# A decoder block in one kernel: a scan and a reciprocal of the WKV tail a slot later, four gaps in SBUF, and a divided last norm

## The reference

```python
x = layernorm(x + attention(x))     # 16 heads of 128, 4 KV heads, RoPE, causal softmax, Wo
x = layernorm(x + wkv(w, u, x, ctx))
x = layernorm(x + ffn(x))

# wkv, per channel, over the positions:
y  = (A * p + E * vt) / (A * q + E)
p, q = A2 * p + E2 * vt, A2 * q + E2

# ffn, per position:
h      = silu(x @ rw1.T + rb1)                      # 64 wide
logits = (h @ rw2.T + rb2)[:, :16] + gates
coeff  = softmax of the two largest logits, 0 elsewhere
out    = x @ W.T + bias + sum over e, r of (x . A[e, r]) * coeff[e] * B[e, :, r]
```

## Time and profile before

| | us |
|---|---|
| runs | 1602.74, 1603.10, 1606.97 (median 1603.1) |
| profiled execution, own time | 1607.82 |
| its span | 1606.0 |
| PE busy | 1556.0 (97%) |
| DVE busy | 1340.3 (83%) |
| ACT busy | 1115.5 (69%) |
| POOL busy | 1007.7 (63%) |
| mean granted TensorE clock | 0.991 |

### The profile page before, as it was taken

One profiled execution on the slowest core, in us unless ns is written; L12 is line 12 of the kernel. 1 busy time (PEld: TensorE's weight loads), 2 busy tenths in 40 slices (PEclk: granted clock), 3 DMA queues, 4 the chain that ended last, 5 costly groups with the idle time before them and its releaser, 6 DMA issues.

```text
span 1606.0 us, 32704 instructions
## 1 busy us (share of the span) xinstructions
PE 1556.0 (97%) x10500; PEld 1413.4 (88%) x10500; DVE 1340.3 (83%) x3434; ACT 1115.5 (69%) x2995; POOL 1007.7 (63%) x850
## 2 busy tenths in 40 slices
PE   8999999999999999999999999999999987989997
PEld 7899999999999999999999999999999976878785
DVE  6776688889888889898999889898989897877863
ACT  6777787877787778777877787878787865334332
POOL 2665586757675867676767666676667653635653
PEclk9999999999999999999999999999999999999999
DMA  9765344324442444244424442445144522121211
GB/s 298 256 225 201 112 150 137 116 73 142 150 137 55 152 146 136 60 152 151 139 60 152 151 139 60 132 146 164 44 126 148 178 70 79 53 93 66 80 66 53
DMA packets 81625, 202.62 MB, mean 126 GB/s; under 512 B 10416, under 2 KB 11056, under 8 KB 81456
## 3 DMA queue, kind: packets, MB, share of 16 engines
q1 hardware_dynamic: 81456, 200.53, 40.0%
HBM read 120.80 MB, written 37.75 MB: 99 GB/s over the span
## 4 chain that ended last, share of the span: by engine, by line
PE 84%; DVE 7%; issue 3%; POOL 2%; ACT 1%; DVEq 1%; DMA 1%; SPq 0%; ACTq 0%; POOLq 0%
PE bank L528 25%; PE bank L529 24%; PE bank L530 24%; PE bank L652 5%; PE bank L597 2%; PE bank L643 1%; PE bank L598 1%; PE bank L635 1%; DVE PS L1328 1%; DVE ED L1339 1%; PE bank L667 1%; DMA SW<-QB 1%; DVE SW L1392 0%; DVE RC L1170 0%; DVE OTl L1243 0%
## 5 line engine op out<-in xcount | busy, mean ns | idle before, releaser
L528 PE MATMUL bank<-Xh,W 128*128 128x256 f32 x1280 | 362.2, 283 | 5.8 <-DVE RC L1170 2.5
L529 PE MATMUL bank<-Xl,W 128*128 128x256 f32 x1280 | 360.5, 282 | 0.0
L530 PE MATMUL bank<-Xh,W 128*128 128x256 f32 x1280 | 360.4, 282 | 0.0
L1025 POOL TENSOR_TENSOR Ql<-RC,Qh 128x512 fp32r<-128x512 f32 x127 | 169.6, 1336 | 208.9 <-ACT Qh L744 208.7
L759 ACT ACTIVATE S<-S,NM 128x128 f32<-128x128 f32 (+1 forms) x512 | 228.2, 447 | 65.8 <-DVE NM L1155 65.2
L528 PEld LDWEIGHTS bank<-Xh,W 128*128 128x128 f32 x1280 | 241.3, 189 | 9.2 <-DVE RC L1170 5.1
L1013 POOL TENSOR_TENSOR SW<-SW,tables 128x512 f32<-128x512 f32 x128 | 170.8, 1334 | 124.6 <-DMA SW<-QB 124.5
L744 ACT ACTIVATE PTh<-bank 128x384 fp32r<-128x384 f32 x256 | 124.9, 488 | 173.1 <-PE bank L652 173.1
L529 PEld LDWEIGHTS bank<-Xl,W 128*128 128x128 f32 x1280 | 241.7, 189 | 0.0
L530 PEld LDWEIGHTS bank<-Xh,W 128*128 128x128 f32 x1280 | 241.6, 189 | 0.0
L744 ACT ACTIVATE S<-S,RL 128x128 f32<-128x128 f32 (+1 forms) x512 | 203.4, 448 | 31.7 <-DVE RL L1162 31.5
(11 more groups left out here) (161 smaller groups left out, 4450.1 us busy)
## 6 DMA issues: line engine op xcount, KB each, us to landing
W<-kept SPq DMA_DIRECT2D x140, 512.0 KB, 4.5
SW<-QB SPq DMA_DIRECT2D x256, 128.0 KB, 2.3
kept<-W SPq DMA_DIRECT2D x40, 512.0 KB, 5.0
XR<-XR SPq DMA_DIRECT2D x64, 128.0 KB, 2.3
RO<-in_xn SPq DMA_DIRECT2D x16, 512.0 KB, 4.1
KVT<-in_ctxt SPq DMA_DIRECT2D x16, 512.0 KB, 4.2
mixed<-RO SPq DMA_DIRECT2D x16, 512.0 KB, 3.8
XR<-in_xt SPq DMA_DIRECT2D x15, 512.0 KB, 4.2
```

The source lines that it names most:

```text
L528: nc.tensor.matmul(dst, lhs[0], rhs[0], start=first, stop=False)
L529: nc.tensor.matmul(dst, lhs[0], rhs[1], start=False, stop=False)
L530: return nc.tensor.matmul(dst, lhs[1], rhs[0], start=False, stop=last)
L1025: gp.tensor_tensor(Q[1][:, :, :], RC[:, i % 2, :, :], Q[0][:, :, :], ALU.subtract).then_inc(q_lo, 1)
```

## The change

Five things are changed.

- One piece of weights (the query weights of head 4, the ninth piece of the first half) is split at slot 2 instead of slot 1.
- `PS_AT[0]` is (11, 0) instead of (10, 1), and the first reciprocal's place is (12, 0) instead of (11, 1), in all 16 tails.
- Four gaps are laid in SBUF, of 64, 64, 64 and 32 bytes in each partition, ahead of X, KHL, Q and PT. Modulo 128 bytes, the start of Xh and Xl moves from 0 to 64, of Q and S from 0 to 64, of PT, OT, RO, KVT and PS from 96 to 64; W, KHL, V, QB, SW, RC and the tables stay at 0 (of QB, SW, RC and KRC the start modulo 256 goes from 0 to 128).
- The last batch's norm is divided by row tile: statistics of tile 0 right behind its sum, scale and shift per tile on POOL, ACT and the store per tile (two DMAs of 256 KB for one of 512 KB).
- The last batch's `logits` is in part 1, right behind the transposes of the hidden values (L713), instead of part 2 behind `dense(1)`.

```diff
-SPLIT_AT = [[-6, -6, -2, -2, -6, -6, 0, 1, 1, 2, 3, 4] + [h // 2 + 4 for h in range(HEADS)],
+SPLIT_AT = [[-6, -6, -2, -2, -6, -6, 0, 1, 2, 2, 3, 4] + [h // 2 + 4 for h in range(HEADS)],
...
-QS_AT, PS_AT, ED_AT = [(8, 0), (10, 0)], [(10, 1), (12, 0)], [(6, 0), (9, 0)]
+QS_AT, PS_AT, ED_AT = [(8, 0), (10, 0)], [(11, 0), (12, 0)], [(6, 0), (9, 0)]
...
+        def gap(i, n):
+            sb(f"gap{i}", [P, n // 4])
+
         XR = sb("XR", [P, KC, T])
         x_raw = lambda b: X1R if b == 1 else XR[:, :, :]
+        gap(0, 64)
         X = [sb(f"X{i}", [P, 2, KC, T], fr) for i in "hl"]
+        gap(1, 64)
...
+        gap(2, 64)
         Q = [sb(f"Q{i}", [P, 2, T], fr) for i in "hl"]
...
+        gap(3, 32)
         PT = [sb(f"PT{i}", [P, 4, P + T], fr) for i in "hl"]
...
# SP, the store
+                    if f < LAST:
...
+                    else:
+                        for t in range(TT):
+                            sp.wait_ge(f_done, f + t + 1)
+                            sp.dma_start(rows[:, t, :], OUT[f % 2][:, t, :]).then_inc(f_out[f % 2], 16)
...
# PE, part 1
                             last = nc.tensor.transpose(bank[4][0:HID, t * P:(t + 1) * P], HE[:, t, :], Ident[:, :])
                         last.then_inc(hid_turned, 1)
+                        if f == LAST:
+                            logits()
                 else:
                     dense(1)
                     turn_x2(1)
...
+                    if stage_of(n, 2) != LAST:
+                        logits()
...
# POOL, scale and shift
+                    for k, those in enumerate((slice(0, 1), slice(1, 2)) if f == LAST else (slice(0, TT),)):
+                        pool.wait_ge(f_ve, f + k + 1)
...
# DVE
-                for tau, c in channels((11, 1), (13, 1), (14, 1), (15, 1)):
+                for tau, c in channels((12, 0), (13, 1), (14, 1), (15, 1)):
...
                     out_sum(3, 0)
+                    if stage_of(n, 3) == LAST:
+                        dve.wait_ge(f_sum, TT * LAST + 1)
+                        dve.wait_ge(f_shift, LAST - 1)
+                        norm_stats(OUT[LAST % 2], LAST % 2, STF, MVF, VEF, f_ve, range(1))
```

More of the change, by code:

```diff
@@ L406, in run @@
                     step(n, part)
+        LAST = BATCH - 1
         def stage_of(n, lag):
@@ L484, in step @@
                 if f is not None and part == 2:
-                    sp.wait_ge(f_done, f + 1)
-                    sp.dma_start(out[TAIL_BATCH[f], :, :].rearrange("(a p) c -> p a c", p=P), OUT[f % 2]).then_inc(f_out[f % 2], 16)
+                    rows = out[TAIL_BATCH[f], :, :].rearrange("(a p) c -> p a c", p=P)
+                    if f < LAST:
+                        sp.wait_ge(f_done, f + 1)
+                        sp.dma_start(rows, OUT[f % 2]).then_inc(f_out[f % 2], 16)
+                    else:
+                        for t in range(TT):
+                            sp.wait_ge(f_done, f + t + 1)
+                            sp.dma_start(rows[:, t, :], OUT[f % 2][:, t, :]).then_inc(f_out[f % 2], 16)
             def load_piece(u):
@@ L522, in _ @@
             for i in range(2):
-                sp.wait_ge(f_out[i], 16 * BATCH // 2)
+                sp.wait_ge(f_out[i], 16 * (BATCH // 2 + (i == LAST % 2)))
         @block.tensor
@@ L668, in turn_x2, with logits @@
                         last.then_inc(f_turned, 1)
+                def logits():
+                    f = stage_of(n, 2)
+                    if f is not None:
+                        pe.wait_ge(hid_copied, f + 1)
+                        for a in range(TT):
+                            last = nc.tensor.matmul(bank[4][:, T + a * EXP:T + (a + 1) * EXP], HST[:, a * P:(a + 1) * P], Rw2, start=True, stop=True)
+                        last.then_inc(logits_done, 1)
                 def dense(t):
@@ L944, in step @@
                     if f is not None:
-                        act.wait_ge(f_shift, f + 1)
                         for t in range(TT):
+                            act.wait_ge(f_shift, f + 1 + t * (f == LAST))
                             last = nc.scalar.activation(OUT[f % 2][:, t, :], OUT[f % 2][:, t, :], ACT.Identity,
                                                         bias=NMF[:, f % 2, t:t + 1], scale=RSF[:, f % 2, t:t + 1])
-                        last.then_inc(f_done, 1)
+                            if f == LAST or t == TT - 1:
+                                last.then_inc(f_done, 1)
                 else:
@@ L1258, in odd, with norm_stats @@
                 tail(n, 0)
-            def norm_stats(tiles, par, stats, mv, ve, done):
-                for t in range(TT):
+            def norm_stats(tiles, par, stats, mv, ve, done, which=range(TT)):
+                for t in which:
                     v.bn_stats(stats[:, par, t, :], tiles[:, t, :])
                 dve.drain()
-                for t in range(TT):
+                for t in which:
                     v.bn_aggr(mv[:, par, t, :], stats[:, par, t, :])
                 dve.drain()
-                v.tensor_scalar(ve[:, par, :], mv[:, par, :, 1], EPS, None, ALU.add).then_inc(done, 1)
+                those = slice(which.start, which.stop)
+                v.tensor_scalar(ve[:, par, those], mv[:, par, those, 1], EPS, None, ALU.add).then_inc(done, 1)
             def norm_shift(par, mv, rs, nm):
@@ L1383, in step @@
                         above(dve, f_shift, f - 1)
-                        norm_stats(OUT[f % 2], f % 2, STF, MVF, VEF, f_ve)
+                        norm_stats(OUT[f % 2], f % 2, STF, MVF, VEF, f_ve, range(f == LAST, TT))
                     f = stage_of(n, 2)
```

11 lines of the change are left out of this document (5 added, 6 removed).

## The result

The change made the kernel faster by three to four times what I had forecast. In the first comparison the median was 1587.01 us (four runs, 1584.7 to 1591.03) beside 1604.68 for the kernel before on the same chip: ratio 0.9892, 95% interval 0.9866 to 0.9918, or 17 us. A second comparison of the same two kernels (`after_again`) gave 1583.60 beside 1607.60: 0.9853 (0.9831 to 0.9876), or 24 us. My 1596.9 was 10 too high, and the range (1588.0 to 1602.5) just missed the first. What came out is near the case that had 0.14, *the gaps pay*.

A forecast was written before the change was run, and what follows sets the result against it. PE was taken as the bound, 84% of the span's chain. Terms -3.6 (heads), +2.4 (last tails), 0 (gaps), -1.9 (logits), -1.7 (half clock), -1.4 (norm), 0 (split) sum to -6.2: 1603.1 to 1596.9 us, range 1588 to 1602.5.

The forecast's parts named there:

- the gaps pay: Rival, chance 0.14: the four SBUF gaps speed matmuls by 1.7 ns each, 9 us on top, so about 1588 us.
- two terms here: Last two tails: +2.4 us (from a 1.08 us PE wait); half-clock stretch behind the last batch's logits gone: -1.7 us.

## What to carry to other kernels

Where TensorE is busy all the time, its pace is a term of the sum, and the start of each operand is a free parameter: divide start-to-start times by family, compare each with the columns at the granted clock, and if a gap is left, move one operand by steps of 32 bytes against the other, for each family by itself. Rows that agree at two places don't price a third. When PE gets faster, read again which engine now is late: PE's own waits for RC went from 0.6 to 5.3 by the gaps alone. And before a term is built on one wait or one half-clock stretch of a trace, look whether another execution of the same work has it: two terms here rested on such rows, and they stand in 2 of 12 and in 4 of 11 traces.

## What the runs showed of the hardware that I had not expected

- The start-to-start time of fp32 matmuls of 256 columns with X moving depended on the distance modulo 256 bytes between the starts of the tiles of their two operands: 114.8 to 115.8 ns at 192, 118 to 120 at 0, 64, 128, 160 and 224; those of 512 columns, with W moving, took 229.2 to 230.5 at 0 and 192, and 232.1 to 234.3 at 32, 64, 96, 128, 160 and 224. Moving both by 64 changed nothing (118.6). For X by W distances of 32 and 96 were not tried, and why it is so stays open. The Trainium skill, "SBUF — State Buffer", section "Who interferes with whom", has TensorE waiting for no other engine; nothing here speaks against that, but these runs show that its two operands are not indifferent to each other.
- One DVE operation (SW<-SW, 128x128) met a POOL operation on 128x512 in the FFN stage of every trace. Where DVE's started first, or POOL's by at most 3 ns, DVE took 0.23 us; where POOL's started 5 to 17 ns ahead, 1.36 to 1.39; where 0.56 to 0.64 us ahead, 0.85 to 0.87. A few nanoseconds decided over 1.1 us. A POOL operation of the same form took 1.41 beside DVE's scan and 0.42 behind it.
- The same idle time of PE, 2.38 to 2.43 us, was followed by 3.4 us at half clock in four traces and by none in seven.
